# One tile of the cross-attention's probabilities turned by VectorE through DRAM instead of by TensorE

## The chip, the cores and the metric

The kernel runs on one core of one Trainium2 chip. The metric is the device time of one execution in microseconds, here the median of three runs. TensorE is called PE below, VectorE DVE, ScalarE ACT, GpSimd POOL and SyncE SP, as in the rows of the profile.

## The reference

A block of three layers on x of shape (64, 32, 512), with a context of shape (64, 257, 384), everything in float32:

```python
x = x + xattn(layernorm(x), context)   # 16 heads of 64: softmax(q k^T / 8) v, then w_o and a bias
x = x + attn(layernorm(x))             # 16 heads of 32, causal, with a decay by distance
x = x + ffn(layernorm(x))              # 512 -> 2048 -> 512, piecewise-linear GELU, rounded to 2^-8
```

The change lies in the first layer. For each of the 64 batches ("contexts"), 16 heads x 32 queries make 512 rows of scores over 257 keys. The kernel computes scores against the context itself (the key weights are folded into the queries), takes the softmax, and mixes the context rows by the probabilities; the value and output weights come behind that.

## The kernel before, in words

All matmuls are in two float32r pieces, a high and a low part of each operand, and three products (high x high, high x low, low x high). Every engine has a program of its own, written out by hand in order; semaphores join them. No scheduler moves anything.

Cross attention goes by groups of eight contexts (`GB = 8`, eight groups). At a group's boundary the queries are projected and the group before gets its value projection. Within it each context b is one turn of the loop on all five engines. Its 512 score rows are four tiles of 128 (`NT = 4`, 16 heads in fours). In one turn:

- PE: `scores(b, 0)` and `scores(b, 1)`, with `turn_probs(b - 1, 1)` between them, `scores(b, 2)`, `scores(b, 3)`, `mix(b - 1, 0)`, `turn_probs(b, 0)`, `mix(b - 1, 1)`, `mix(b - 1, 2)`. `turn_probs(b, half)` (L911) turns two tiles of probabilities by four 128x128 transposes into a PSUM bank; `mix` (L926) takes the turned probabilities `probt` as one operand. The first, second and last context of a group have a slightly different order.
- DVE: `top` (maximum of a score tile, L1283), `invert` (reciprocal of its sum, L1291), `turn_context` (L1260: 32x32 block transposes of the next context, which lie in `blocks_in`), the low parts of the turned context, of the probabilities (`low_probs`, L1296) and of the mix.
- ACT: the exponentials (`exponent`, L1096) and the high parts (`high_turned`, `high_probs`, `high_mix`, `high_context`).
- POOL: `low_context` (L786), `scale` (L791: multiplies a tile of exponentials by its reciprocal, in place), `shift` (L780), and in five contexts of a group the split of one 128x512 block of the FFN's weights (L797 to L801), which goes through DRAM (`ffn`).
- SP issues every transfer: `load_context` (L613), `load_odd` (L619), the FFN blocks (L639 to L650), and `load_blocks` (L603): four reads that bring the context's 32x32 blocks to where DVE's block transpose makes a full transpose of them. `load_blocks(b + 2)` is issued in turn b and used by DVE's `turn_context(b + 2, 0)` in turn b + 1, right behind `top(b + 1, 0)`.

SP's order in a turn is written in this loop:

```python
if b + 2 < B:
    load_context(b + 2)
for j in ffn_block_of(b + 1) if b % GB == 0 else ffn_block_of(b) if b % GB > 1 else ():
    load_ffn_block(j)
if b + 2 < B:
    if b % GB > 0:
        load_blocks(b + 2)
    load_odd(b + 2)
```

## Time and profile before

| | |
|---|---|
| median of three runs | 1588.15 us (1588.05 to 1588.57) |
| the profiled execution | 1588.07 us |
| its span in the profile | 1586.2 us |
| PE busy | 1570.0 us, 99% |
| DVE, ACT, POOL busy | 1243.0, 1020.1, 816.3 us |
| granted PE clock | full speed over the whole span (2.4 GHz) |

The span is the time from the first to the last instruction; some 2 us of the execution lie around it. A timeline row gives the start in us from the span's start, the duration in us, the engine, the line and the operation; neighbours of one kind are merged (x4) and the idle time before stands in square brackets where there was some. PE's matmuls are pipelined, so durations overlap and the distance between starts is what one takes. Cross attention's groups run from about 110 to 900 us of the span.

### The profile page before, as it was taken

The page shows a single profiled execution, that of the slowest core. Times are in us where ns is not written, and L with a number is a line of the kernel's source. Part 1 is how long each engine was busy: PE and PEld are TensorE (multiplying, and loading weights), DVE is VectorE, ACT ScalarE, POOL GpSimd, SP SyncE. Part 2 cuts the span into 40 slices and gives each one's busy share as a digit, 9 for nine tenths or more (in the row PEclk, how much of TensorE's full clock was granted, in tenths as well). Part 3 has the DMA queues.
Part 4 walks back from the last instruction along what each step waited for, and adds up shares of the span by engine and source line. Part 5 has one row for each costly group of instructions (what it writes and reads, how often), then busy time and mean ns, then how long its engine had stood idle before and what let it go on. Part 6 is the DMA issues. An engine that isn't in the chain of part 4 may idle for free. (4 is left out here: it accounts for less than half of the span.)

```text
span 1586.2 us, 30382 instructions
## 1 busy us (share of the span) xinstructions
PE 1570.0 (99%) x11114; PEld 1376.8 (87%) x11114; DVE 1243.0 (78%) x2411; ACT 1020.1 (64%) x2025; POOL 816.3 (51%) x780
## 2 busy tenths in 40 slices
PE   9999999999999999999999999999999999999998
PEld 7889899898999989999899888988988887888886
DVE  6558878787888878878788685767777889989887
ACT  3457777777777777777787442445446666676765
POOL 3317657376573856747455232334334555555554
PEclk9999999999999999999999999999999999999999
DMA  8984636456364654635443684432436601010010
GB/s 253 273 256 150 179 112 186 128 168 178 116 185 120 179 164 128 184 111 151 140 111 95 188 285 138 133 93 80 137 94 228 238 14 61 20 43 31 14 48 27
DMA packets 203412, 215.60 MB, mean 136 GB/s; under 512 B 83776, under 2 KB 149632, under 8 KB 203264
## 3 DMA queue, kind: packets, MB, share of 16 engines
q1 hardware_dynamic: 203264, 213.66, 44.3%
q8 instruction: 89, 1.46, 0.4%
q14 instruction: 59, 0.48, 0.1%
HBM read 154.88 MB, written 58.72 MB: 135 GB/s over the span
## 5 line engine op out<-in xcount | busy, mean ns | idle before, releaser
L79 PE MATMUL p_bank_score<-p_ctxt,p_qo 128*128 128x256 f32 x2304 | 304.5, 286 | 0.7 <-ACT p_probs L1105 0.3
L79 PEld LDWEIGHTS p_bank_score<-p_ctxt,p_qo 128*128 128x128 f32 x2304 | 288.1, 191 | 5.8 <-issue 2.1
L79 PE MATMUL p_bank_mix<-p_probt,p_ctx 128*128 128x512 f32 x1152 | 292.1, 398 | 0.5
L79 PEld LDWEIGHTS p_bank_mix<-p_probt,p_ctx 128*128 128x128 f32 x1152 | 207.4, 189 | 41.9 <-issue 3.8
L1307 DVE SCALAR_TENSOR_TENSOR p_qo<-p_bank_mix,p_odd,p_qo 128x512 fp32r<-128x512 f32 x192 | 143.8, 749 | 57.7 <-ACT p_qo L1119 50.1
L1119 ACT ACTIVATE p_qo<-p_bank_mix,p_odd 128x512 fp32r<-128x512 f32 x192 | 132.3, 689 | 68.1 <-PE p_bank_mix L79 67.7
L1105 ACT ACTIVATE p_probs<-p_bank_score,p_small 128x257 f32<-128x257 f32 x256 | 121.3, 475 | 59.6 <-DVE p_small L1288 55.6
L794 POOL TENSOR_SCALAR p_probs<-p_probs,p_small 128x256 f32<-128x256 f32 x256 | 121.4, 480 | 71.3 <-DVE p_small L1294 71.2
L788 POOL TENSOR_TENSOR p_ctx<-p_ctx_in,p_ctx 128x768 fp32r<-128x768 f32 x64 | 118.3, 1848 | 68.1 <-ACT p_ctx L1094 67.7
L783 POOL TENSOR_TENSOR p_ctx_in<-p_ctx_in,p_odd_in 128x768 f32<-128x768 f32 x64 | 118.1, 1846 | 40.7 <-DMA p_odd_in<-in_ctx_dram 40.7
L1288 DVE TENSOR_REDUCE p_small<-p_bank_score 128x1 f32<-128x257 f32 x256 | 105.3, 414 | 10.7 <-PE p_bank_score L79 7.9
L79 PE MATMUL p_bank_mm<-p4a_zt,p_wattn 128*128 128x256 f32 x768 | 96.0, 285 | 0.5 <-PEq L1454 0.3
L1278 DVE SCALAR_TENSOR_TENSOR p_ctxt<-p_bank_turn,p_odd_minus,p_ctxt 128x256 fp32r<-128x256 f32 x192 | 87.0, 481 | 12.1 <-ACT p_ctxt L1084 11.7
L79 PEld LDWEIGHTS p_bank_mm<-p4a_zt,p_wattn 128*128 128x128 f32 x768 | 93.0, 191 | 1.8 <-issue 0.5
L1837 POOL TENSOR_TENSOR p_pieces_k<-p_pieces_k 128x512 f32<-128x512 f32 (+1 forms) x33 | 52.5, 1591 | 75.8 <-ACT p_pieces_k L2060 75.8
L1084 ACT ACTIVATE p_ctxt<-p_bank_turn,p_odd_minus 128x256 fp32r<-128x256 f32 x192 | 83.5, 470 | 10.5 <-DVE p_bank_turn L1272 8.3
L771 POOL CAST p_qo<-p_probs 128x512 fp32r<-128x512 f32 x32 | 19.5, 610 | 134.6 <-ACT p_probs L1142 134.6
L1837 POOL TENSOR_TENSOR p_pieces_q<-p_pieces_q 128x512 f32<-128x512 f32 x32 | 52.1, 1629 | 69.4 <-ACT p_pieces_q L2060 69.4
L1272 DVE STREAM_TRANSPOSE p_bank_turn<-p_blocks_in 128x256 f32<-128x256 f32 x192 | 78.6, 440 | 3.2 <-DMA p_blocks_in<-in_ctx_dram 2.9
L1301 DVE TENSOR_TENSOR p_probt<-p_bank_probt,p_probt 128x512 fp32r<-128x512 f32 x112 | 75.6, 675 | 0.2
L79 PE MATMUL p_bank_mm<-p5a_zt,p_wattn 128*128 128x512 f32 x288 | 71.5, 397 | 0.0
L949 PE MATMUL p_bank_score<-p_qo,p_wv 128*64 128x256 f32 x312 | 70.1, 284 | 0.6
(302 smaller groups left out, 3910.7 us busy)
## 6 DMA issues: line engine op xcount, KB each, us to landing
p_blocks_in<-in_ctx_dram SPq DMA_DIRECT2D x256, 96.0 KB, 2.4
p_ctx_in<-in_ctx_dram SPq DMA_DIRECT2D x64, 384.0 KB, 3.2
q<-p_ctx SPq DMA_DIRECT2D x64, 256.0 KB, 3.6
ffn<-p_w_raw SPq DMA_DIRECT2D x64, 256.0 KB, 3.0
p_odd_in<-in_ctx_dram SPq DMA_DIRECT2D x64, 192.0 KB, 3.6
p_x<-in_x_dram SPq DMA_DIRECT2D x32, 256.0 KB, 4.2
p_quad<-q SPq DMA_DIRECT2D x32, 256.0 KB, 3.7
p_probt<-q SPq DMA_DIRECT2D x32, 256.0 KB, 3.9
```

Source lines behind the costliest of these rows:

```text
L79: made = e.matmul(out, lhsT, rhs, start=n == 0, stop=n == last)
L783: e.tensor_tensor(ctx_in[b % 2][:], ctx_in[b % 2][:], odd_in[:, None, :].to_broadcast([P, SP, CC]), ALU.subtract).then_inc(shifted, 1)
L788: e.tensor_tensor(ctx[b % 2][:, LO], ctx_in[b % 2][:], f32(ctx[b % 2][:, HI]), ALU.subtract).then_inc(ctx_lo, 1)
L794: e.tensor_scalar(probs[n % 6][:, 0:KEYS], probs[n % 6][:, 0:KEYS], small[n % 4][:, 2:3], 1.0, ALU.mult, ALU.mult).then_inc(normal, 1)
L1084: e.activation(ctxt[b % 2][:, HI, k, :], b_turn[:, (k % 2) * KEYS:(k % 2 + 1) * KEYS], ACT.Identity, bias=odd_minus[:, k, b:b + 1]).then_i ...
L1105: e.activation(probs[n % 6], b_score[n % NS][:, 0:S], ACT.Exp, bias=small[n % 4][:, 0:1], accum_out=small[n % 4][:, 1:2]).then_inc(exped, 1)
L1119: e.activation(qo[:, HI, m, b % GB, :, :].rearrange("p h t -> p (h t)"), b_mix[m], ACT.Identity, bias=odd[:, m, b:b + 1]).then_inc(out_hi, 1)
L1272: e.transpose(b_turn[:, (k % 2) * KEYS:(k % 2 + 1) * KEYS].rearrange("p (i c) -> p i c", c=QUAD), blocks_in[:, :, k, :]).then_inc(turned, 1)
L1278: e.scalar_tensor_tensor(out=ctxt[b % 2][:, LO, k, :], in0=b_turn[:, (k % 2) * KEYS:(k % 2 + 1) * KEYS], scalar=odd_minus[:, k, b:b + 1], ...
L1288: e.tensor_reduce(small[n % 4][:, 0:1], b_score[n % NS][:, 0:S], AX, ALU.max, negate=True).then_inc(topped, 1)
L1307: e.scalar_tensor_tensor(out=lo, in0=b_mix[m], scalar=odd[:, m, b:b + 1], in1=f32(hi), op0=ALU.add, op1=ALU.subtract).then_inc(out_lo, 1)
L1837: e.tensor_tensor(a[:, at], a[:, at], g0[:, at], ALU.subtract).then_inc(sloped, 1)
```

## The change

In the second to seventh context of each group (`is_moved`, 48 of 64) tile 0 of the probabilities is no longer turned by PE. `scale(b, 0)` writes it, with its columns in another order, to a buffer (`moving`, which lies over the low half of `probt`). SP puts it to DRAM (`put_rows`), waits for that to land, and reads it back in four transfers (`move_blocks`) that bring its 32x32 blocks to where one DVE block transpose (`turn_moved`) makes a full transpose of them, in the next context's turn. ACT takes its high part (`high_moved`) and POOL its low part (`low_moved`). PE's `turn_probs` does only tile 1 in half 0, and `mix` takes its six products in another order, the ones with the low probabilities last, behind a wait of their own. `move_blocks(b)` stands ahead of `load_blocks(b + 2)` in SP's program.

```diff
         def sync(e):
...
+            def put_rows(b):
+                e.wait_ge(normal, b * NT + 1)
+                e.dma_start(p_dram[b % 2], moved_from(b)).then_inc(rows_put, DMA)
+
+            def move_blocks(b):
+                e.wait_ge(rows_put, DMA * moves(b))
+                for q in range(NQD):
+                    e.dma_start(moved_to(b)[q * QUAD:(q + 1) * QUAD, :].rearrange("r (h n) -> r h n", h=HT),
+                                p_dram[b % 2, :, q * SP * QUAD:(q + 1) * SP * QUAD].rearrange(
+                                    "(h r) n -> r h n", r=QUAD)).then_inc(blocks_moved, DMA)
...
                     for j in ffn_block_of(b - 1) if b % GB > 0 else ():
                         store_ffn_block(j)
+                    if is_moved(b):
+                        put_rows(b)
                     if b + 2 < B:
                         load_context(b + 2)
                     for j in ffn_block_of(b + 1) if b % GB == 0 else ffn_block_of(b) if b % GB > 1 else ():
                         load_ffn_block(j)
+                    if is_moved(b):
+                        move_blocks(b)
                     if b + 2 < B:
                         if b % GB > 0:
                             load_blocks(b + 2)
...
         def gpsimd(e):
...
+                to, made = probs[n % 6][:, 0:KEYS], probs[n % 6][:, 0:KEYS]
+                if tile == 0 and is_moved(b):
+                    e.wait_ge(mixed, KC * (b - 1))
+                    to = moved_from(b).rearrange("p (q s k) -> p s q k", s=SP, k=QUAD)
+                    made = made.rearrange("p (s q k) -> p s q k", s=SP, k=QUAD)
+                e.tensor_scalar(to, made, small[n % 4][:, 2:3], 1.0, ALU.mult, ALU.mult).then_inc(normal, 1)
+
+            def low_moved(b):
+                e.wait_ge(moved_hi, moves(b))
+                e.tensor_tensor(probt[b % 2][:, LO, :, 0:P], turned_to(b), f32(probt[b % 2][:, HI, :, 0:P]),
+                                ALU.subtract).then_inc(moved_lo, 1)
...
                 low_context(b)
+                if is_moved(b - 1):
+                    low_moved(b - 1)
...
         def tensor(e):
...
-                for i in range(2):
+                for i in (1,) if half == 0 and is_moved(b) else (0, 1):
...
-                    e.wait_ge(probt_lo, 2 * (b + 1))
+                    e.wait_ge(probt_hi, 2 * (b + 1))
+                    if is_moved(b):
+                        e.wait_ge(moved_hi, moves(b))
...
+                for h in (HI, LO):
+                    for s in range(SP):
+                        e.matmul(b_mix[m], ctx[i][:, h, s, cols], probt[i][:, HI, s, :], start=h == HI and s == 0,
+                                 stop=False)
+                if m == 0:
+                    e.wait_ge(probt_lo, 2 * (b + 1))
+                    if is_moved(b):
+                        e.wait_ge(moved_lo, moves(b))
+                for s in range(SP):
+                    made = e.matmul(b_mix[m], ctx[i][:, HI, s, cols], probt[i][:, LO, s, :], start=False,
+                                    stop=s == SP - 1)
...
         def scalar(e):
...
+            def high_moved(b):
+                e.wait_ge(blocks_turned, moves(b))
+                e.activation(probt[b % 2][:, HI, :, 0:P], turned_to(b), ACT.Copy).then_inc(moved_hi, 1)
...
                     exponent(b, 0)
+                    if is_moved(b - 1):
+                        high_moved(b - 1)
...
         def vector(e):
...
+            def turn_moved(b):
+                e.wait_ge(blocks_moved, DMA * NQD * moves(b))
+                e.transpose(turned_to(b).rearrange("p s (h r) -> p h s r", r=QUAD),
+                            moved_to(b).rearrange("p (h s k) -> p h s k", s=SP, k=QUAD)).then_inc(blocks_turned, 1)
...
                     else:
+                        if is_moved(b - 1):
+                            turn_moved(b - 1)
                         if not first:
                             low_probs(b - 1, 1)
```

How it moves the instructions on SP, in one ordinary context's turn. Before (L648 and L650 store an FFN block, L616 is `load_context`, L644 `load_ffn_block`, L609 `load_blocks`, L622 `load_odd`):

```order
L648 DMA ffn<-p2_w_raw1 128x512
L650 DMA ffn<-p2_w_raw0 128x512
L616 DMA p2_ctx_in1<-in_ctx_768_dram 128x2x384
L644 DMA p2_w_raw0<-in_L0_ffn_w1_dram 128x512
L609 DMA p2_blocks_in<-in_ctx_768_dram 32x8x96 x4
L622 DMA p2_odd_in<-in_ctx_768_dram 128x384
```

And with the change, where the lines are those of the changed kernel (L679 and L681 the stores, L685 `put_rows`, L690 `move_blocks`, L640 `load_blocks`):

```order
L679 DMA ffn<-p2_w_raw1 128x512
L681 DMA ffn<-p2_w_raw0 128x512
L685 DMA p<-p2_moving0 128x256
L647 DMA p2_ctx_in0<-in_ctx_768_dram 128x2x384
L675 DMA p2_w_raw0<-in_L0_ffn_w1_dram 128x512
L690 DMA p2_probs<-p 32x4x64 x4
L640 DMA p2_blocks_in<-in_ctx_768_dram 32x8x96 x4
L653 DMA p2_odd_in<-in_ctx_768_dram 128x384
```

The put stands ahead of the context's load, and the four reads of the moved blocks stand between the FFN block's load and the four block loads of the next context but one.

On DVE, from the first maximum of a turn on, before (L1272 is `turn_context`, L1301 `low_probs`, L1288 `top`, L1294 `invert`):

```order
L1288 TENSOR_REDUCE p2_small0<-p2_bank_score 128x1
L1272 STREAM_TRANSPOSE p2_bank_turn<-p2_blocks_in 128x256 x2
L1301 TENSOR_TENSOR p2_probt1<-p2_bank_probt,p2_probt1 128x2x256
L1288 TENSOR_REDUCE p2_small1<-p2_bank_score 128x1
L1294 RECIPROCAL p2_small0<-p2_small0 128x1
L1278 SCALAR_TENSOR_TENSOR p2_ctxt1<-p2_bank_turn,p2_odd_minus,p2_ctxt1 128x256 x2
L1288 TENSOR_REDUCE p2_small2<-p2_bank_score 128x1
L1294 RECIPROCAL p2_small1<-p2_small1 128x1
```

And with the change (L1348, L1377, L1364 and L1370 are the same four, L1381 is `turn_moved`):

```order
L1364 TENSOR_REDUCE p2_small0<-p2_bank_score 128x1
L1348 STREAM_TRANSPOSE p2_bank_turn<-p2_blocks_in 128x256 x2
L1381 STREAM_TRANSPOSE p2_moving0<-p2_probs 128x4x2x32
L1377 TENSOR_TENSOR p2_probt0<-p2_bank_probt,p2_probt0 128x2x256
L1364 TENSOR_REDUCE p2_small1<-p2_bank_score 128x1
L1370 RECIPROCAL p2_small0<-p2_small0 128x1
L1354 SCALAR_TENSOR_TENSOR p2_ctxt0<-p2_bank_turn,p2_odd_minus,p2_ctxt0 128x256 x2
L1364 TENSOR_REDUCE p2_small2<-p2_bank_score 128x1
L1370 RECIPROCAL p2_small1<-p2_small1 128x1
```

One more block transpose stands between `turn_context` and `low_probs`, and everything behind it comes later by as much.

On POOL, the first instructions of a turn, with the change (L834 is `low_context`, L849 `low_moved`, L845 `scale`, L829 `shift`):

```order
L834 TENSOR_TENSOR p2_ctx0<-p2_ctx_in0,p2_ctx0 128x768
L849 TENSOR_TENSOR p2_probt1<-p2_moving1,p2_probt1 128x2x128
L845 TENSOR_SCALAR p2_moving0<-p2_probs,p2_small0 128x2x4x32
L845 TENSOR_SCALAR p2_probs<-p2_probs,p2_small1 128x256
L829 TENSOR_TENSOR p2_ctx_in1<-p2_ctx_in1,p2_odd_in 128x768
```

The low part of the tile that was moved in the last turn stands between `low_context` and this turn's first `scale`, where nothing stood before.

## Rows read from the trace of the kernel before

**Rows 1.** The page: busy time by engine, and one group of part 5.

```profile
PE 1570.0 (99%) x11114; PEld 1376.8 (87%) x11114; DVE 1243.0 (78%) x2411; ACT 1020.1 (64%) x2025; POOL 816.3 (51%) x780
...
L922 PE MATMUL p_bank_probt<-ident,p_probs 128*128 128x128 f32 x448 | 67.0, 272 | 0.0
```

**Rows 2.** Timeline of PE: start us, us, engine, line, operation, count.

```profile
527.03 1.24 PE L79 MATMUL p_bank_score<-p_ctxt,p_qo 128*128 128x256 f32 x9
528.11 0.60 PE L922 MATMUL p_bank_probt<-ident,p_probs 128*128 128x128 f32 x4
528.47 3.47 PE L79 MATMUL p_bank_score<-p_ctxt,p_qo 128*128 128x256 f32 x27
531.77 1.55 PE L79 MATMUL p_bank_mix<-p_probt,p_ctx 128*128 128x512 f32 x6
533.17 0.60 PE L922 MATMUL p_bank_probt<-ident,p_probs 128*128 128x128 f32 x4
533.52 2.99 PE L79 MATMUL p_bank_mix<-p_probt,p_ctx 128*128 128x512 f32 x12
536.35 1.24 PE L79 MATMUL p_bank_score<-p_ctxt,p_qo 128*128 128x256 f32 x9
```

**Rows 3.** Timeline of DVE in the same context.

```profile
528.96 0.78 DVE L1272 STREAM_TRANSPOSE p_bank_turn<-p_blocks_in 128x256 f32<-128x256 f32 x2
529.64 0.67 DVE L1301 TENSOR_TENSOR p_probt<-p_bank_probt,p_probt 128x512 fp32r<-128x512 f32 x1
530.24 0.42 DVE L1288 TENSOR_REDUCE p_small<-p_bank_score 128x1 f32<-128x257 f32 x1
530.58 0.15 DVE L1294 RECIPROCAL p_small<-p_small 128x1 f32<-128x1 f32 x1
```

**Rows 4.** Timeline of ACT in the same context.

```profile
529.83 0.84 ACT L1084 ACTIVATE p_ctxt<-p_bank_turn,p_odd_minus 128x256 fp32r<-128x256 f32 x2
530.75 0.48 ACT L1105 ACTIVATE p_probs<-p_bank_score,p_small 128x257 f32<-128x257 f32 x1
```

**Rows 5.** Timeline of POOL, from the group's second context on.

```profile
521.27 0.49 POOL L794 TENSOR_SCALAR p_probs<-p_probs,p_small 128x256 f32<-128x256 f32 x1
...
526.38 0.61 POOL L799 CAST p_w_raw<-p_w_raw 128x512 fp32r<-128x512 f32 x1
527.08 1.30 POOL L801 TENSOR_TENSOR p_w_raw<-p_w_raw 128x512 fp32r<-128x512 f32 x1
528.73 1.84 POOL L788 TENSOR_TENSOR p_ctx<-p_ctx_in,p_ctx 128x768 fp32r<-128x768 f32 x1 [0.36 <-ACT p_ctx L1094]
530.83 0.48 POOL L794 TENSOR_SCALAR p_probs<-p_probs,p_small 128x256 f32<-128x256 f32 x1 [0.25 <-DVE p_small L1294]
532.07 0.48 POOL L794 TENSOR_SCALAR p_probs<-p_probs,p_small 128x256 f32<-128x256 f32 x1 [0.77 <-DVE p_small L1294]
```

**Rows 6.** Timeline of SP's DMA issues (merged, x4 is four issues).

```profile
530.61 0.38 SPq L616 DMA_DIRECT2D p_ctx_in<-in_ctx_dram  x1
...
532.86 1.81 SPq L609 DMA_DIRECT2D p_blocks_in<-in_ctx_dram  x4
```

**Rows 7.** DMA landings: block loads over the span, the last in context 3, one w_raw load.

```profile
DMA to landing us min/median/max: 2.0/2.4/6.6
...
DMA to landing us min/median/max: 2.5/2.6/2.6
...
p_w_raw<-in_L_ffn_w_dram SPq DMA_DIRECT2D x1, 256.0 KB, 4.2
```

**Rows 8.** Timeline of SP in stage two: a row tile put and read back.

```profile
1012.21 0.34 SPq L1703 DMA_DIRECT2D z<-p4a_z  x1
1014.26 1.75 SPq L1712 DMA_DIRECT2D p4a_z<-z  x4
1025.09 0.34 SPq L1703 DMA_DIRECT2D z<-p4a_z  x1
...
1027.83 1.75 SPq L1712 DMA_DIRECT2D p4a_z<-z  x4
```

More of the change, by code:

```diff
@@ L243, in __init__, with cross_attention @@
         self.late_in = room.sem_ring("late_in", 3)
-def cross_attention(nc, kept, stack, ident, ident_ready, x_rows, w_q, w_k, w_v, w_o, b_o, ctx_dram, q_dram, o_dram,
+def cross_attention(nc, kept, stack, ident, ident_ready, x_rows, w_q, w_k, w_v, w_o, b_o, ctx_dram, q_dram, p_dram, o_dram,
                     x1_dram, moments, w_attn, w_proj, w_1, w_2, ffn_dram):
@@ L307, in cross_attention @@
             ctxt = [carve(second, f"ctxt{i}", [P, 2, KC, KEYS], F32R) for i in range(2)]
+            with ExitStack() as between:
+                carve(between, "probt0_high", [P, SP, ROW])
+                moving = [carve(between, "moving0", [P, SP, ROW])]
             probt = [carve(second, "probt0", [P, 2, SP, ROW], F32R)]
+            with ExitStack() as between:
+                carve(between, "probt1_high", [P, SP, ROW])
+                moving.append(carve(between, "moving1", [P, SP, ROW]))
             with ExitStack() as boundaries:
@@ L374, in probs_bank, with is_moved, moves, moved_from @@
             return b_probt
+        def is_moved(b):
+            return 0 < b % GB < GB - 1
+        def moves(b):
+            return b // GB * (GB - 2) + b % GB
+        def moved_from(b):
+            return moving[b % 2][:, 0, 2 * P:2 * P + KEYS]
+        def moved_to(b):
+            return probs[b * NT % 6][:, 0:KEYS]
+        def turned_to(b):
+            return moving[b % 2][:, :, 0:P]
         FIRST_TWO = [(b, 1 + 4 * b) for b in range(2)]
+        def probs_rows(b, half, side):
+            first = P if half == 0 and is_moved(b) else 0
+            return (probt[b % 2][:, side, :, half * 2 * P + first:(half + 1) * 2 * P],
+                    probs_bank(b, half).rearrange("p (s r) -> p s r", s=SP)[:, :, first:2 * P])
         def turned_in(b):
@@ L410, in cross_attention @@
             "probs_turned", "probt_hi", "probt_lo", "mixed", "out_hi", "out_lo")
+        rows_put, blocks_moved, blocks_turned, moved_hi, moved_lo = room.sems(
+            "rows_put", "blocks_moved", "blocks_turned", "moved_hi", "moved_lo")
         queried, qo_hi, qo_lo, qo_mid, qo_pool, valued, o_half, o_whole = room.sems(
@@ L793, in scale @@
                 e.wait_ge(inverted, n + 1)
-                e.tensor_scalar(probs[n % 6][:, 0:KEYS], probs[n % 6][:, 0:KEYS], small[n % 4][:, 2:3], 1.0,
-                                ALU.mult, ALU.mult).then_inc(normal, 1)
+                to, made = probs[n % 6][:, 0:KEYS], probs[n % 6][:, 0:KEYS]
[8 more added lines that the diff above has]
+                                ALU.subtract).then_inc(moved_lo, 1)
             def split_ffn_block(j):
@@ L934, in mix @@
                     e.wait_ge(out_lo, KC * (b - 1) + m + 1)
-                accumulate(e, b_mix[m], [x for s in range(SP) for x in three(
-                    lambda h, s=s: ctx[i][:, h, s, cols], lambda h, s=s: probt[i][:, h, s, :])]
-                ).then_inc(mixed, 1)
+                for h in (HI, LO):
[9 more added lines that the diff above has]
+                                    stop=s == SP - 1)
+                made.then_inc(mixed, 1)
             def add_values(g, t, i, side, ks, bank):
@@ L1099, in exponent @@
                     e.wait_ge(probs_turned, (n - 6) // 2 + 1)
+                if n >= 6 and (n - 6) % NT == 0 and is_moved((n - 6) // NT):
+                    e.wait_ge(blocks_turned, moves((n - 6) // NT))
                 if tile == 0 and b > 0 and b % GB == 0:
@@ L1113, in high_probs @@
                 e.wait_ge(probs_turned, 2 * b + half + 1)
-                e.activation(probt[b % 2][:, HI, :, half * 2 * P:(half + 1) * 2 * P],
-                             probs_bank(b, half).rearrange("p (s r) -> p s r", s=SP), ACT.Copy).then_inc(probt_hi, 1)
+                hi, bank = probs_rows(b, half, HI)
+                e.activation(hi, bank, ACT.Copy).then_inc(probt_hi, 1)
+            def high_moved(b):
+                e.wait_ge(blocks_turned, moves(b))
+                e.activation(probt[b % 2][:, HI, :, 0:P], turned_to(b), ACT.Copy).then_inc(moved_hi, 1)
             def high_mix(b, m):
@@ L1299, in low_probs @@
                     e.wait_ge(o_gone[0], DMA * NT // 2 * (b // GB))
-                hi, lo = (probt[b % 2][:, s, :, half * 2 * P:(half + 1) * 2 * P] for s in (HI, LO))
-                e.tensor_tensor(lo, probs_bank(b, half).rearrange("p (s r) -> p s r", s=SP), f32(hi),
-                                ALU.subtract).then_inc(probt_lo, 1)
+                (hi, bank), (lo, _) = (probs_rows(b, half, s) for s in (HI, LO))
+                e.tensor_tensor(lo, bank, f32(hi), ALU.subtract).then_inc(probt_lo, 1)
+            def turn_moved(b):
+                e.wait_ge(blocks_moved, DMA * NQD * moves(b))
+                e.transpose(turned_to(b).rearrange("p s (h r) -> p h s r", r=QUAD),
+                            moved_to(b).rearrange("p (h s k) -> p h s k", s=SP, k=QUAD)).then_inc(blocks_turned, 1)
             def low_mix(b, m):
@@ L2374, in build @@
     q_dram = nc.dram_tensor("q", [2, INNER, ROWS], F32, kind="Internal").ap()
+    p_dram = nc.dram_tensor("p", [2, P, (S - 1) // P * P], F32, kind="Internal").ap()
     o_dram = nc.dram_tensor("o", [INNER, ROWS], F32, kind="Internal").ap()
@@ L2390, in build @@
                 nc, kept, weights, ident, ident_ready, x_rows, L0_xattn_w_q, L0_xattn_w_k, L0_xattn_w_v, L0_xattn_w_o, L0_xattn_b_o,
-                ctx_768, q_dram, o_dram, x1_dram, x1_moments, L0_attn_w_attn, L0_attn_w_proj, L0_ffn_w1, L0_ffn_w2, ffn_dram)
+                ctx_768, q_dram, p_dram, o_dram, x1_dram, x1_moments, L0_attn_w_attn, L0_attn_w_proj, L0_ffn_w1, L0_ffn_w2, ffn_dram)
             after = FirstProducts(nc, kept, ident, ident_ready, x2_moments)
```

## Prediction

> **What bounds the kernel now.** I read the page first. PE is busy 99% of the span, VectorE 78%, ScalarE 64%, GpSimd 51% [rows 1]: the kernel is as long as PE's instruction stream, and a change helps only if it shortens that stream without making PE wait. Then I read the timeline of one ordinary context, the third of a group, engine by engine, because shares say nothing about which wait is near. PE starts its scores at 527.03 and those of the next context at 536.35 [rows 2]: the pitch is **9.32 us** and PE has no hole in it. What matters is how closely the others follow. VectorE turns the next context's blocks at 528.96, runs low_probs at 529.64, the maximum of tile 1 at 530.24 and the reciprocal of tile 0 at 530.58, with no gap [rows 3]. ScalarE's high_turned starts at 529.83 and the exponential of tile 1 at 530.75 [rows 4]. GpSimd scales tile 0 from 530.83 to 531.31 and tile 1 until 532.55 [rows 5]; PE turns tile 1 at 533.17 [rows 2], so that chain has **0.62 us** of slack. SyncE issues the context's block loads at 532.86, four in 1.81 us [rows 6], and the last lands 2.6 us after its issue [rows 7]: 532.86 + 1.36 (three quarters of 1.81) + 2.6 = 536.8. VectorE needs them one pitch after 528.96, at 538.28. This transfer has 1.5 us of slack, and the change moves work in front of it.
>
> **What PE is rid of.** 48 contexts (six in each of eight groups) lose the two PE transposes of tile 0. Four of them take 528.47 - 528.11 = 0.36 us and 533.52 - 533.17 = 0.35 us from first start to next start [rows 2], so one is worth 0.089 us: 96 x 0.089 = **8.5 us** off PE's stream. The group's row offers two larger values: 67.0 us over 448 is 150 ns, and the mean of one is 272 ns [rows 1]; both count overlap with the neighbours, and the start-to-start time is what PE gives back. The mix does the same six matmuls in another order, and its later wait for the low halves can only help: cost nothing, hidden in the same stream.
>
> **What the others get, beside PE's stream.** VectorE: one more 128x256 transpose, 0.34 us to the next start (0.78 for two, so one lasts 0.44) [rows 3]; low_probs of half 0 is halved and comes late in the context, where it delays nobody, so I count nothing back. ScalarE: high_moved, 256 wide, about 0.47 by the 257-wide exponential's 0.48 [rows 4]. GpSimd: low_moved, a two-input operation 256 wide; 768 wide takes 1.84 and 512 wide 1.30 [rows 5], so 0.54 for each 256 elements and 0.76 for the one. Its bounds are 0.48 (the one-input scale of that width) and 0.92 (half of 1.84). Effect within a context, even if every transfer is early: blocks turned 0.68 + third transpose 0.44 + 0.09 to ScalarE (530.66 to 530.75 [rows 3, 4]) + high_moved 0.47, then high_turned 0.84 and a gap of 0.03, puts tile 1's exponential 2.55 us after VectorE's 528.96 instead of 1.79. Those 0.76 us meet the 0.62 us of slack: 0.14 us is left over. Small, but the slack is gone, so any further lateness of VectorE goes straight to PE.
>
> **What SyncE gets: a loop.** In each of the 48 contexts SyncE now waits for tile 0's scale, puts the rows to DRAM, issues the context and FFN loads, waits until the put has *landed*, issues four moved-block reads, and only then the four block loads that VectorE needs early in the next context. There VectorE's work leads to the next scale of tile 0. So each context starts where the last one's block loads landed. Step by step, from the end of scale(b, 0):
> - to the put's issue: 0.04 (ctx_lo at 530.57, SyncE at 530.61 [rows 5, 6]).
> - put's issue to the first read's: in stage two a tile is put and read back in just this form, 1012.21 to 1014.26 = 2.05 us, and 1025.09 to 1027.83 = 2.74 us behind another load [rows 8]. Here the queue is nearly empty ahead of the put: I take 2.05, with 2.74 as the other end. The context and FFN issues, some 0.4 us each [rows 6], fit inside it.
> - four reads issued: 1.75 [rows 8] plus a gap of 0.05: 1.80; bounds 1.4 (four of 0.34 [rows 8]) and 1.86 (as rows 6).
> - the fourth block load starts 1.36 after the first [rows 6] and lands 2.6 after that [rows 7]; bounds 2.0 (the smallest of all) and 4.2 (a load that was queued behind a context load) [rows 7]. Then 0.05 to VectorE.
> That is 0.04 + 2.05 + 1.80 + 1.36 + 2.60 + 0.05 = **7.90 us** from scale to blocks. From there VectorE turns blocks 0.68, moved rows 0.44, 0.09, high_moved 0.47, 0.07, low_moved 0.76, scale 0.48 [rows 3 to 5]: **2.99 us** (the 0.09 is the gap read above; 0.07 and the 0.05s are estimates for gaps of its kind). Low_moved stands ahead of scale in GpSimd's program, so all of it counts; the path through low_probs, maximum and reciprocal (0.68 + 0.34 + 0.60 + 0.34 + 0.15 and 0.1 to GpSimd = 2.2) is shorter than the 2.5 in front of scale. One turn of the loop: 7.90 + 2.99 = **10.89 us** against a pitch of 9.32: 1.57 us too long.
>
> Over a group: the loop starts in the second context, whose scale ends at 521.76 [rows 5]; VectorE wants the blocks at 528.96, 7.20 us later, and gets them after 7.90: 0.70 late. Five more turns (third to seventh context's scale, then the blocks for the eighth's) add 5 x 1.57: 8.55 us. VectorE has no slack left, so PE is late by as much, plus the 0.14 of above: 8.7 us. PE never catches up, since its stream is dense; and the 8.5 us of transposes it no longer does only lengthen its waits. In the last group no blocks are left to load in the seventh context, one turn fewer. Sum: 8 x 8.7 - 1.57 = **68 us**.
>
> The Trainium skill ("DMA: Bandwidth & Descriptors", Anatomy of one DMA) gives a transfer about 2.0 us plus its bytes over 436 GB/s. By it the 128 KB put would take 2.3 us and a 96 KB block load 2.2 us, an estimate by which the turn is 10.74 us and the sum some 61 us. The rows have 2.05 for a put of 256 KB and 2.6 for the loads; the sum above goes by the rows.
>
> The profiled execution took 1588.07 us (span 1586.2), 0.08 below the median of 1588.15; 1588.07 + 68 = **1656**.
>
> **The rivals.**
> 1. *PE stays the bound: faster.* If the turn came out at 9.13 us or less (pitch less 0.18), nothing would wait and PE would keep the 8.5 us: **1580**. The put and the reads would have to be nearly two microseconds quicker than rows 7 and 8 have them. For it: VectorE, ScalarE and GpSimd all have idle time in total. Against it: the smallest value of each row still makes 0.04 + 2.05 + 1.4 + 1.36 + 2.0 + 0.05 + 2.71 = 9.61. Chance 0.08. The Trainium skill ("TensorE: Matmul & The Clock Gate", Part 4: PE-mode transpose) gives a PE transpose about 275 ns in a kernel; if all of that came back this case would be 96 x 0.275 = 26 us and 1562 us, an estimate; rows 2 speak against it.
> 2. *GpSimd's loop decides: slower by less.* The FFN block load now stands behind the put: issued 0.82 after scale (0.04, the put's 0.34 [rows 8], the context load's 0.38 [rows 6], gaps), landed 4.2 later [rows 7], then cast and difference 2.0 (0.70 and 1.30), low_context 1.84, low_moved 0.76, scale 0.48 [rows 5] and 0.05: 10.15 us a turn. It decides where the block loads land in 2.0 and low_moved takes 0.48. Some 26 turns (four per group, 6.4 groups, since 32 blocks go five to a group) x 0.83 = 21 us: **1609**. Chance 0.15.
> 3. *The transfers collide: slower by more.* With the put at 2.74, because the context and FFN loads (640 KB) follow on its heels, the turn is 11.58 and the first lateness 1.39: 8 x (1.39 + 5 x 2.26 + 0.14) - 2.26 = 100 us: **1688**. Block loads behind the moved reads at 4.2 as well would make 13.2 a turn and about 1760. Chance 0.20.
> 4. *No change.* The 8.5 us and a turn of some 9.5 us cancel: **1588**. Chance 0.02. That the edit does not act is excluded by the order of instructions on SyncE and VectorE.
>
> **How the numbers follow.** Forecast 0.55 at 1656; rivals 0.08, 0.15, 0.20 and 0.02. The range leaves out the faster case and the far end of the third: from 1605, just under rival 2, to 1700, just over rival 3 at the put's measured bound. A measurement of this kernel can tell about 0.2%, 3 us. Faster: 0.08; within: 0.02; slower: 0.55 + 0.15 + 0.20 = 0.90.
>
> **What would show it.** PE's idle time, 16 us now (1586.2 less 1570.0 [rows 1]), grows to 80 to 90 us, in front of the transposes of tile 1 (and some in front of the mix). VectorE's transposes of blocks_in wait for a DMA, 45 us or more in total. SyncE waits at the moved reads for the put, about 1 us in each of 48. Within a group, contexts two to seven run at a pitch of 10.9 us, and the first and last keep theirs. Wrong would be: pitch at or under 9.3 (rival 1), GpSimd's cast waiting for w_raw in every turn (rival 2), a put over 2.6 us (rival 3). If VectorE waits for the moved reads instead of the block loads, the loop is another one than I describe.

## The result and the profile after

The changed kernel takes **1655.23 us** (median of four runs, 1654.22 to 1656.01) beside 1588.19 for the kernel before on the same chip: ratio **1.0421, 95% interval [1.0408, 1.0434]**, slower by 67 us. The prediction was 1656, 68 us more. The profiled execution took 1654.82 us, its span is 1653.0.

The page's part 1 of the changed kernel, answering to [rows 1]:

```profile
PE 1576.9 (95%) x11018; PEld 1366.6 (83%) x11018; DVE 1249.2 (76%) x2459; ACT 1016.1 (61%) x2073; POOL 851.4 (52%) x828
```

PE has 96 matmuls fewer and is 76.1 us idle instead of 16.2. It is even 6.9 us *busier*. The last matmul ahead of a stall is shown with its whole tail, 0.15 us or so of which otherwise lies under the next one. PE stalls 73 times in the two rows below, so that is some 11 us (an estimate). Against experiment 2, which runs the same matmuls without these stalls and has PE busy for 1564.2 us, it is 12.7 us more. So 59.9 us more of idle time and 6.9 us more of busy time make the 66.8 us of span. Where it waits, and who makes it wait (view of the waits: engine, line, releaser, us in total, times, longest):

```profile
ACT p_probt L1189 <- DVE p_moving L1381: 84.0, 47, 3.8
DVE p_bank_turn L1348 <- DMA p_blocks_in<-in_ctx_dram: 68.5, 48, 3.4
POOL p_probt L849 <- ACT p_probt L1189: 61.4, 47, 3.5
PE p_bank_probt L979 <- POOL p_probs L845: 37.4, 47, 0.9
PE p_bank_mix L996 <- ACT p_probt L1189: 22.0, 26, 2.4
```

Read it from the bottom: PE waits 37.4 us for the scale of tile 1 ahead of its transposes and 22.0 us for high_moved ahead of the mix. Both stand behind the second row: VectorE's turn of the context waits for the block loads, 48 times, 68.5 us. It never waits for the moved rows: the view has no such row for `turn_moved` (L1381), and in the turn below it starts right behind the turn of the context.

One turn of the loop, first SyncE (start, duration, line):

```profile
576.35 0.32 SPq L685 DMA_DIRECT2D p<-p_moving  x1
576.72 0.43 SPq L647 DMA_DIRECT2D p_ctx_in<-in_ctx_dram  x1
577.20 0.49 SPq L675 DMA_DIRECT2D p_w_raw<-in_L_ffn_w_dram  x1
578.09 1.75 SPq L690 DMA_DIRECT2D p_probs<-p  x4
579.89 2.62 SPq L640 DMA_DIRECT2D p_blocks_in<-in_ctx_dram  x4
```

then VectorE and GpSimd:

```profile
584.60 0.79 DVE L1348 STREAM_TRANSPOSE p_bank_turn<-p_blocks_in 128x256 f32<-128x256 f32 x2 [1.77 <-DMA p_blocks_in<-in_ctx_dram]
585.29 0.40 DVE L1381 STREAM_TRANSPOSE p_moving<-p_probs 128x256 f32<-128x256 f32 x1
```

```profile
575.84 0.48 POOL L845 TENSOR_SCALAR p_moving<-p_probs,p_small 128x256 f32<-128x256 f32 x1
...
586.22 0.73 POOL L849 TENSOR_TENSOR p_probt<-p_moving,p_probt 128x256 fp32r<-128x256 f32 x1 [1.65 <-ACT p_probt L1189]
586.94 0.47 POOL L845 TENSOR_SCALAR p_moving<-p_probs,p_small 128x256 f32<-128x256 f32 x1
```

The scale ends at 576.32, SyncE puts it at 576.35, the blocks are there at 584.60, 8.28 us later; the next scale ends at 587.41, 2.81 us after that. PE waits twice in this turn, 0.67 us for high_moved ahead of the mix and 0.88 us for the scale of tile 1. With the two tails that is 1.85 us, by which the turn (11.09) is longer than PE's stream of 9.24 (experiment 2):

```profile
580.82 1.24 PE L79 MATMUL p_bank_score<-p_ctxt,p_qo 128*128 128x256 f32 x9
...
586.40 1.17 PE L996 MATMUL p_bank_mix<-p_probt,p_ctx 128*128 128x512 f32 x4 [0.67 <-ACT p_probt L1189]
...
588.91 0.41 PE L979 MATMUL p_bank_probt<-ident,p_probs 128*128 128x128 f32 x2 [0.88 <-POOL p_probs L845]
...
591.91 1.24 PE L79 MATMUL p_bank_score<-p_ctxt,p_qo 128*128 128x256 f32 x9
```

PE's scores of this group's contexts start at 559.51, 570.56, 580.82, 591.91, 602.45 and 613.53: pitches of 11.05, 10.26, 11.09, 10.54 and 11.08, mean 10.80, where it was 9.32. The group's second context takes 8.15 us (8.32 before): the block loads are late only from the first put on.

### The profile page after: what moved, and what is told of

The parts are those of the page before. It is cut to its first block and busy times, and to the rows that moved or that the text cites. A ratio compares the mean times of both kernels' runs of the same rounds, so it can differ in the third digit from the quotient of the medians.

```text
span 1653.0 us, 30718 instructions
## 1 busy us (share of the span) xinstructions
PE 1576.9 (95%) x11018; PEld 1366.6 (83%) x11018; DVE 1249.2 (76%) x2459; ACT 1016.1 (61%) x2073; POOL 851.4 (52%) x828
## 5 line engine op out<-in xcount | busy, mean ns | idle before, releaser
L996 PE MATMUL p_bank_mix<-p_probt,p_ctx 128*128 128x512 f32 x768 | 216.6, 404 | 22.1 <-ACT p_probt L1189 22.0
L1387 DVE SCALAR_TENSOR_TENSOR p_qo<-p_bank_mix,p_odd,p_qo 128x512 fp32r<-128x512 f32 x192 | 143.8, 749 | 46.6 <-ACT p_qo L1193 36.7
L829 POOL TENSOR_TENSOR p_ctx_in<-p_ctx_in,p_odd_in 128x768 f32<-128x768 f32 x64 | 118.1, 1846 | 45.1 <-DMA p_odd_in<-in_ctx_dram 45.1
L834 POOL TENSOR_TENSOR p_ctx<-p_ctx_in,p_ctx 128x768 fp32r<-128x768 f32 x64 | 118.3, 1848 | 40.6 <-ACT p_ctx L1162 40.3
L1348 DVE STREAM_TRANSPOSE p_bank_turn<-p_blocks_in 128x256 f32<-128x256 f32 x192 | 79.1, 442 | 68.8 <-DMA p_blocks_in<-in_ctx_dram 68.5
L845 POOL TENSOR_SCALAR p_probs<-p_probs,p_small 128x256 f32<-128x256 f32 x208 | 98.9, 484 | 61.9 <-DVE p_small L1370 61.9
L1003 PE MATMUL p_bank_mix<-p_probt,p_ctx 128*128 128x512 f32 x384 | 118.9, 391 | 0.0
L1364 DVE TENSOR_REDUCE p_small<-p_bank_score 128x1 f32<-128x257 f32 x256 | 104.2, 412 | 7.3 <-PE p_bank_score L79 7.2
L979 PE MATMUL p_bank_probt<-ident,p_probs 128*128 128x128 f32 x352 | 59.5, 277 | 37.4 <-POOL p_probs L845 37.4
L1919 POOL TENSOR_TENSOR p_pieces_k<-p_pieces_k 128x512 f32<-128x512 f32 (+1 forms) x33 | 52.6, 1594 | 75.8 <-ACT p_pieces_k L2142 75.8
L979 PEld LDWEIGHTS p_bank_probt<-ident,p_probs 128*128 128x128 f32 x352 | 39.5, 140 | 58.2 <-issue 51.5
```

What stands on the lines that cost most here:

```text
L829: e.tensor_tensor(ctx_in[b % 2][:], ctx_in[b % 2][:], odd_in[:, None, :].to_broadcast([P, SP, CC]), ALU.subtract).then_inc(shifted, 1)
L834: e.tensor_tensor(ctx[b % 2][:, LO], ctx_in[b % 2][:], f32(ctx[b % 2][:, HI]), ALU.subtract).then_inc(ctx_lo, 1)
L979: made = e.transpose(bank[:, at:at + P], probs[n % 6][:, s * P:(s + 1) * P], ident[:])
L996: e.matmul(b_mix[m], ctx[i][:, h, s, cols], probt[i][:, HI, s, :], start=h == HI and s == 0, stop=False)
L1003: made = e.matmul(b_mix[m], ctx[i][:, HI, s, cols], probt[i][:, LO, s, :], start=False, stop=s == SP - 1)
L1364: e.tensor_reduce(small[n % 4][:, 0:1], b_score[n % NS][:, 0:S], AX, ALU.max, negate=True).then_inc(topped, 1)
```

## Experiments

Ratios are against the kernel before, run on the same chip beside each. "The change" is the changed kernel.

**1. The block loads ahead of the moved reads.** The loop is cut: the block loads no longer stand behind the put's landing.

```diff
+                    if b + 2 < B and b % GB > 0:
+                        load_blocks(b + 2)
                     if is_moved(b):
                         move_blocks(b)
                     if b + 2 < B:
-                        if b % GB > 0:
-                            load_blocks(b + 2)
                         load_odd(b + 2)
```

> SyncE's four block loads stand ahead of the four moved reads; everything else is the change. Theory (a loop from scale over the put, the moved reads and the block loads to the next scale): the blocks are issued 1.5 us after scale, land 5.6 after it, 1.6 before VectorE asks, and the loop over them is gone. The moved reads land about 7.0 after scale, just in time: about 1588 us, 1580 to 1598, the waits of VectorE for blocks_in under 5 us (68.5 in the change). Rival (the added work of VectorE, ScalarE and GpSimd, or the added traffic, makes PE wait): over 1640. Rival (GpSimd's loop over the FFN block's load): about 1600, with GpSimd's cast waiting for w_raw in four contexts of a group.

Measured: 1618.53 us, ratio 1.0191 [1.0177, 1.0205]. Over half of the loss comes back, not all. VectorE still waits for blocks, 22.3 us instead of 68.5, and GpSimd's cast now waits 29.1 us for the FFN block. The block loads are issued 1.45 us after the put (567.42 to 568.87) instead of 3.55 (566.09 to 569.64 in the change), but they land later than the 2.4 us at the median of [rows 7] (landings of the block loads over the span):

```profile
DMA to landing us min/median/max: 2.0/3.5/7.6
```

The put's loop was the larger half. That it was all of it, as I expected, was wrong.

**2. Everything but the transfers.** Put and reads are left out, and turn_moved turns what lies in the buffer.

```diff
-                    if is_moved(b):
-                        put_rows(b)
...
-                    if is_moved(b):
-                        move_blocks(b)
...
-                e.wait_ge(blocks_moved, DMA * NQD * moves(b))
+                e.wait_ge(normal, b * NT + 1)
```

> The put and the moved reads are left out; VectorE turns the tile as it stands (not normalized, not blocked), so the probabilities of tile 0 are not the reference's in 48 contexts. All the work that the change adds to VectorE, ScalarE and GpSimd stays, and SyncE's program is that of before. Theory (the loop through SyncE is the whole loss): PE gets back the 8.5 us, less 0.14 us in a context: 1580 to 1587 us. Rival (added engine work in VectorE's dense stretch): each context loses a microsecond, 1630 or more.

Measured: 1587.08 us, 0.9993 [0.9983, 1.0002]; the pitch in the middle of a group:

```profile
524.26 1.24 PE L79 MATMUL p_bank_score<-p_ctxt,p_qo 128*128 128x256 f32 x9
...
533.50 1.24 PE L79 MATMUL p_bank_score<-p_ctxt,p_qo 128*128 128x256 f32 x9
...
542.73 1.24 PE L79 MATMUL p_bank_score<-p_ctxt,p_qo 128*128 128x256 f32 x9
```

9.24: the 9.32 of before, less 0.18 for two transposes, plus 0.10 for the work that VectorE, ScalarE and GpSimd got (predicted 0.14). So the engines' new work uses up most of the 8.5 us that PE gives back (1.1 us is left, just above the range of 1580 to 1587 that I had named), but it costs nothing against the kernel before. The 67 us come with the transfers and their place in SyncE's program.

**3. The put stays, the reads don't wait for it.** They fetch rows of the context instead, so what is turned is not the probabilities.

```diff
             def move_blocks(b):
-                e.wait_ge(rows_put, DMA * moves(b))
...
-                                p_dram[b % 2, :, q * SP * QUAD:(q + 1) * SP * QUAD].rearrange(
+                                ctx_dram[b, 0:P, q * SP * QUAD:(q + 1) * SP * QUAD].rearrange(
```

> The put goes out as in the change, but the four moved reads fetch rows of the context input instead, so they need not wait for the put's landing (the probabilities of tile 0 are not the reference's in 48 contexts). Theory (the loop is made of SyncE's issues and the last landing; SyncE is busy issuing during most of the put's flight): only 0.42 us in the four contexts with an FFN load and some 0.9 in the other two come back, 8 x 3.5 = 28 us: 1622 to 1636. Rival (the round trip of the put is what costs): 1.75 us a context, 1590 or less.

Measured: 1636.29 us, 1.03 [1.0286, 1.0314]. Without the wait for the landing 19 us come back, the upper edge of my range. In the turn above the context and FFN issues end at 577.69 and the reads start at 578.09, so SyncE waits only 0.4 us for the put. That holds for the 25 turns with an FFN load; in the other 23 fewer issues cover the put, and it waits about 0.95 us. The view of SyncE's own waits in the changed kernel sums it up:

```profile
SPq L690 <- DMA p<-p_moving: 33.1, 47, 2.1
```

So 33 us of waiting are gone and only 19 us of time come back. I haven't shown where the other 14 go. In this run GpSimd's cast waits 21.5 us for the FFN block instead of 12.9. VectorE still waits 50.8 us for the block loads, since the issues alone keep them late.

**4. The mix's new order alone, in the kernel before.**

```diff
-                    e.wait_ge(probt_lo, 2 * (b + 1))
+                    e.wait_ge(probt_hi, 2 * (b + 1))
...
+                for h in (HI, LO):
+                    for s in range(SP):
+                        e.matmul(b_mix[m], ctx[i][:, h, s, cols], probt[i][:, HI, s, :], start=h == HI and s == 0,
+                                 stop=False)
```

> The kernel before with nothing but the mix's new order of products and its later wait for the low halves. Theory (as predicted: it costs nothing): 1588.2 within 1 us. Rival (another order of operands costs PE, 0.07 us a product group as the distance between starts after a wait suggests): 192 x 0.05 = 10 us slower.

Measured: 1587.78 us, 0.9997 [0.9988, 1.0006]. It costs and brings nothing.

**5. SyncE's part alone, in the kernel before.** PE still turns all four tiles; the put of tile 0, the wait for it to land and four reads of a quarter of its columns into a spare tile are added ahead of the block loads. The reads have 1.75 us of issue time, as in the change.

```diff
+                    if is_moved(b):
+                        put_rows(b)
                     if b + 2 < B:
                         load_context(b + 2)
...
+                    if is_moved(b):
+                        move_blocks(b)
```

> The kernel before, PE turning all four tiles, with SyncE's part alone added: the put of tile 0, and four reads of it (a quarter of the columns, into a spare tile that nobody reads) ahead of the block loads. Theory (SyncE's order closes the loop without any of the added engine work): the turn is 7.5 to 8.3 us from scale to blocks plus 2.35 through turn_context, low_probs, maximum, reciprocal and scale, some 10.2 us against 9.32: 1618 to 1640 us. Rival (the loss needs the added work of VectorE, ScalarE and GpSimd): 1588 to 1592.

Measured: 1635.9 us, 1.0304 [1.0289, 1.0319] and VectorE waits 75.8 us for the block loads, 47 times. Five DMA issues and two waits (for the scale and for the put's landing) ahead of the block loads cost 48 us with no added engine work. The block loads themselves are no slower: they land in 2.5 us at the median here and in 2.4 in the changed kernel, where it was 2.4 before. They are issued too late.

**6. Every other context moved** (contexts 1, 3 and 5 of a group, 24 instead of 48).

```diff
         def is_moved(b):
-            return 0 < b % GB < GB - 1
+            return b % GB in (1, 3, 5)
```

> The change with only the second, fourth and sixth context of a group moved (24, not 48), SyncE in the order of the change. Theory (a loop: a late block load makes the next scale, and with it the next put, late): the loop is cut after every turn, VectorE is late by 0.3 to 1.1 us once per moved context and starts anew: 1600 to 1615 us. Rival (each moved context costs the same by itself): half of the 67 us, 1622.

Measured: 1611.01 us, 1.0148 [1.013, 1.0165]: 23 us. Half the contexts cost a third of the loss; the same price for each moved context would be half, 1622 us. I had 1600 to 1615 for a loop that starts anew after each.

**7, 8. What holds the block loads back once the loop is cut?** Both start from experiment 1. First with the put behind the context and FFN loads, then also with the engines' new work moved off the way to tile 1.

```diff
-                    if is_moved(b):
-                        put_rows(b)
                     if b + 2 < B:
                         load_context(b + 2)
                     for j in ffn_block_of(b + 1) if b % GB == 0 else ffn_block_of(b) if b % GB > 1 else ():
                         load_ffn_block(j)
+                    if is_moved(b):
+                        put_rows(b)
```

and in 8, on VectorE (ScalarE and GpSimd alike):

```diff
-                        if is_moved(b - 1):
-                            turn_moved(b - 1)
                         if not first:
                             low_probs(b - 1, 1)
                         top(b, 1)
+                        if is_moved(b - 1):
+                            turn_moved(b - 1)
```

> As e1_blocks_first, and the put stands behind the context load and the FFN block's load instead of ahead of them. Theory (what was left of e1's loss is GpSimd's loop: its cast waited up to 3.5 us for w_raw, which was issued behind the put and landed after 4.0 us and more in a burst of ten transfers): the FFN load goes out 0.8 us earlier, GpSimd's cast waits under 0.3 us, the block loads land in 3.0 or less: 1588 to 1600 us. Rival (the added traffic as such fills the DMA engines): no better than e1, 1612 or more, with the block loads still at 3.5.

> As e5, and the added work stands where each engine has room: turn_moved behind the maximum of tile 1, high_moved behind the exponential of tile 1, low_moved between the scales of tile 0 and tile 1. Theory (the 0.76 us that the added work puts in front of tile 1's exponential uses up the 0.62 us of slack): PE waits for no scale and the pitch is 9.13 where the transfers are in time: 1580 to 1588 us, faster than before. Rival (the transfers bound it): the same as e5.

Measured: 1623.46 us, 1.0231 [1.0205, 1.0256], and 1626.55 us, 1.0237 [1.0221, 1.0253]. Neither is better than experiment 1. The put now lands in 3.1 us (1.7 ahead of the loads), and the load of an FFN block now waits for the stores of the one before to land, with the block loads behind it (waits of SP's queue, first of these two kernels; in the kernel before they are 5.0 us in 7 and in the changed one 0.9 in 2):

```profile
SPq L675 <- DMA ffn<-p_w_raw: 64.0, 25, 3.9
```

So the edit brought another landing wait in front of the block loads, and neither run can tell what held them back in experiment 1. The block loads land in 2.7 us at the median here, not 3.5, and VectorE still waits for them, 21.2 and 29.0 us. That made me suspect SyncE's own time: in the turn of the changed kernel above the issues of the put, the four reads, the four block loads and the FFN, context and odd rows take 6.0 us, with two stores 7.1.

**9, 10. The four reads issued by ScalarE,** in two gaps of its program, and no longer by SyncE; in 10 with the engines' new work placed as in 8.

```diff
                         high_mix(b - 1, 0)
                         high_probs(b, 0)
...
+                    if is_moved(b):
+                        move_blocks(b, 0)
                     if not first:
                         high_mix(b - 1, 1)
+                        if is_moved(b):
+                            move_blocks(b, 1)
                         high_mix(b - 1, 2)
```

> The four reads of the moved rows are issued from ScalarE's program, two behind high_probs(b, 0) and two behind high_mix(b - 1, 1), where ScalarE stood idle for 0.62 and 0.68 us in the kernel before; everything else is the change. SyncE keeps the put alone (0.33 us). Theory (what is left of the loss once the loop is open is SyncE's own issue time, not the traffic): block loads are issued some 0.4 us later than before, inside their 1.5 us of slack, VectorE never waits for them, and 1584 to 1594 us come out, since turn_moved still stands ahead of low_probs. Rival (the traffic itself: more transfers in flight make every landing slower, whoever issues them): block loads land in 3.5 us and more as in the runs with the block loads first, VectorE waits for them 20 us or more, 1610 to 1625.

> The same with turn_moved behind the maximum of tile 1, high_moved behind the exponential of tile 1 and low_moved between the scales of tiles 0 and 1, so that nothing new stands on the way to tile 1's exponential. Theory (SyncE's issue time): the 8.5 us of transposes begin to show, 1579 to 1587 us, PE's pitch 9.15 to 9.25 us. Rival (traffic): as the run without the reordering, 1610 to 1625, and PE waits in front of the mix instead of in front of the transposes.

Measured: 1646.74 us, 1.0368 [1.0352, 1.0383], and 1628.17 us, 1.0248 [1.0234, 1.0262]. My theory falls; both are even above the range that its rival had. SyncE and ScalarE of experiment 10:

```profile
571.46 1.91 SPq L640 DMA_DIRECT2D p_blocks_in<-in_ctx_dram  x4
```

```profile
572.28 0.31 ACTq L1182 DMA_DIRECT2D p_probs<-p  x1
...
572.62 0.46 ACTq L1182 DMA_DIRECT2D p_probs<-p  x1
...
573.60 0.79 ACTq L1182 DMA_DIRECT2D p_probs<-p  x2
```

```profile
577.70 0.79 DVE L1351 STREAM_TRANSPOSE p_bank_turn<-p_blocks_in 128x256 f32<-128x256 f32 x2 [0.94 <-DMA p_blocks_in<-in_ctx_dram]
```

The block loads are issued 1.4 us after the scale's end (570.06), as soon as VectorE has left their buffer, and still VectorE gets them at 577.70, 4.3 us after the last one's issue has ended (573.37). The reads of the other queue went out beside them. Landings by kind in experiment 10, from 300 to 800 us (KB each, median us; before: 2.4, 3.5 and 3.6 for the first three rows shown):

```profile
p_blocks_in<-in_ctx_dram SPq DMA_DIRECT2D x152, 96.0 KB, 3.8
...
p_odd_in<-in_ctx_dram SPq DMA_DIRECT2D x39, 192.0 KB, 4.4
p_w_raw<-in_L_ffn_w_dram SPq DMA_DIRECT2D x22, 256.0 KB, 4.0
...
p_probs<-p ACTq DMA_DIRECT2D x116, 32.0 KB, 3.9
```

Against 9, experiment 10 also shows what the order of the engines is worth when the moved rows come late: in 9 high_moved stands ahead of tile 1's exponential and waits for turn_moved with all of ScalarE behind it (73.9 us in 47, up to 3.0). In 10 that is 3.9 us in 5.

**11, 12. Packets or neighbours?** Both start from experiment 10. In 11 the reads fetch the same bytes in a quarter of the pieces; in 12 the 384 KB of the context load go behind the block loads.

```diff
-                e.dma_start(moved_to(b)[q * QUAD:(q + 1) * QUAD, :].rearrange("r (h n) -> r h n", h=HT),
-                            p_dram[b % 2, :, q * SP * QUAD:(q + 1) * SP * QUAD].rearrange(
-                                "(h r) n -> r h n", r=QUAD)).then_inc(blocks_moved, DMA)
+                e.dma_start(moved_to(b)[q * QUAD:(q + 1) * QUAD, :],
+                            p_dram[b % 2, q * QUAD:(q + 1) * QUAD, :]).then_inc(blocks_moved, DMA)
```

```diff
-                    if b + 2 < B:
-                        load_context(b + 2)
...
                         if b % GB > 0:
                             load_blocks(b + 2)
+                        load_context(b + 2)
                         load_odd(b + 2)
```

> The reordered run with the reads on ScalarE, but each of the four reads fetches 32 whole rows of 1 KB instead of 128 pieces of 256 B (the same bytes; the tile so arrives in another order than the transpose needs, so what is turned is not the probabilities). Theory A (it is the number of small packets: the run before had 576 more per context on top of 1968, and its block loads took 3.8 us where they take 2.4 without them): block loads land in 2.4 to 3.0 us again and 1582 to 1600 us come out. Theory B (it is the bytes in flight, or the instants at which the transfers meet): block loads stay at 3.5 us or more and the time stays within 8 us of 1628.

> The reordered run with the reads on ScalarE, and load_context (384 KB, needed only a turn later) issued behind the four block loads instead of ahead of them. Theory A (packets in flight ahead of and beside the block loads make them land late, 3.8 us instead of 2.4): with a third of what is in flight out of the way the block loads land in 2.5 to 3.2 us, the FFN load in 3.3 or less, and 1585 to 1605 us come out. Theory B (the two queues are served in turns, whatever stands ahead): the block loads still meet the four reads, stay at 3.5 us or more, and 1620 to 1632 us come out.

Measured: 1616.88 us, 1.018 [1.0165, 1.0195], and 1606.14 us, 1.0107 [1.009, 1.0124]. In 11 the block loads still take 3.6 us at the median of the span (3.7 in experiment 10). The 11 us gained lie between its two ranges, so the number of pieces plays a part, though not in these loads' median: PE's wait for high_moved ahead of the mix falls from 36.7 to 26.8 us. In 12 the block loads take 2.7 and VectorE hardly waits for them any more (waits from 110 to 900 us):

```profile
PE p_bank_mix L986 <- ACT p_probt L1187: 19.9, 28, 2.0
DVE p_moving L1383 <- DMA p_probs<-p: 14.2, 16, 2.1
DVE p_bank_turn L1350 <- DMA p_blocks_in<-in_ctx_dram: 2.2, 5, 0.7
POOL p_w_raw L844 <- DMA p_w_raw<-in_L_ffn_w_dram: 2.0, 4, 0.7
```

The context load ahead of them was most of the second limit, 22 of 40 us; the time is 1 us above what theory A of 12 named (1585 to 1605). What is left is PE's wait for high_moved, 19.9 us in 28 turns (first row). One part of it is that VectorE now waits for the moved reads themselves, 14.2 us in 16 turns; they land in 3.3 us at the median. Another shows on ScalarE, in a good turn and the next:

```profile
562.97 0.79 ACTq L1181 DMA_DIRECT2D p_probs<-p  x2
...
572.26 1.74 ACTq L1181 DMA_DIRECT2D p_probs<-p  x2
...
574.05 0.69 ACT L1191 ACTIVATE p_qo<-p_bank_mix,p_odd 128x512 fp32r<-128x512 f32 x1 [1.10 <-PE p_bank_mix L993]
```

The two issues take 1.74 us instead of 0.79, and what ScalarE has to do behind them is late by 0.4 us (the mark names PE; the issues that end at 574.00 are what the row starts behind). PE's pitch is 9.29 in the turn with the short issue (564.15 to 573.44) and 9.67 in the one with the long (to 583.11), and PE waits 0.34 us for high_moved in it.

No version beats the kernel before: 1606.14 is the best that computes everything, and 1587.08 without any transfer is the same as before.

## Why the prediction was right, point by point

- *The loop is the mechanism.* Experiment 5 makes 48 of the 67 us in a kernel that is otherwise the one before; experiment 2 has all the rest of the change and loses nothing; cutting the loop (1) gives 37 us back. The block loads land in 2.4 us at the median before and after, so in the changed kernel it is their issue that is late. PE's two waits, 37.4 and 22.0 us, are all but 0.5 of its 59.9 us more of idle time. Rival 1, PE as the bound, is refuted by the pitch (10.80 for 9.13 or less), and rival 4, no change, by the time.
- *The term of 7.90 us from scale to blocks.* In two neighbouring turns it is 7.45 and 8.28, and over 47 turns 7.43 to 9.94, mean 8.08: about half of them near 7.5, the others over 8. The put's issue to the first read is 1.74 (576.35 to 578.09), not 2.05, since the put of 128 KB lands in 1.7, where the rows I took were of 256 KB. Rival 3's 2.74 came up in one turn of 48 (2.93; another had 2.52), though the context and FFN loads follow on its heels. The four reads' issue to the block loads' is 1.80, as said. The issue of the four block loads is 1.91 in most turns and 2.4 to 3.4 in 13, where I had 1.81 in every turn; in other turns they land later. So the put was 0.3 too long in my sum, and the block loads' issue and landing were up to 1 us and more too short in half of the turns.
- *The term of 2.99 us from blocks to scale.* 2.81 in the turn shown and within 0.02 of it in all: turn_moved and high_moved start 0.44 apart, low_moved takes 0.73, the scale 0.47. So the turn of 10.89 is met as 8.08 + 2.82 = 10.90: the mechanism is the one forecast, but that the sum is met within 0.01 is luck, since its terms are off by 0.2 to 0.4 both ways.
- *Turn and group.* Mean pitch 10.80 for 10.89, in turns that alternate, which I had not foreseen. From the last scores of one group to those of the next: 509.27 to 614.95 in the changed kernel, 105.7 us, and 477.59 to 575.10 before, 97.5. The seven such distances add 7.5 to 10.5 us each, on average 8.7, as predicted.
- *The sum by the Trainium skill's rule* ("DMA: Bandwidth & Descriptors", Anatomy of one DMA: about 2.0 us plus bytes over 436 GB/s), some 61 us. That section fits its figures to transfers that GpSimd issues, which the prediction leaves out; here SyncE issues them. The trace does not agree with it: the put landed in 1.7 us where the rule gives 2.3, and the block loads in 2.0 to 6.7 (median 2.4) where it gives 2.2. The measured 67 us are nearer to the sum by the rows.
- *Costed at nothing.* The mix's order (experiment 4) and, nearly, the engines' work (experiment 2: 0.10 us a context for 0.14).
- *Rival 2, GpSimd's loop,* is not the longer one but shows: the cast waits 12.9 us in 24 turns for its block, and once the put's loop is cut (experiment 1) it waits 29.1 us, longer than VectorE for the block loads (22.3 us). The prediction's condition for this rival was not right: low_moved stands in both loops, so a shorter one shortens GpSimd's as well (9.87 us against 10.01 with its numbers), and the rival would not have decided.
- *PE's waits* were said to come ahead of the transposes of tile 1 (37.4 us) with some ahead of the mix (22.0); idle time 76 us where I said 80 to 90. The 16.2 of before and the 66.8 of span make 83.0, and the 6.9 us by which PE is busier are the difference. SyncE's wait for the put is 0.4 us in the turns with an FFN load and 0.95 in the others, 0.7 on average, where I named 1 us: I had costed the context and FFN issues inside the put's time, but not subtracted them here.

What I had wrong came after: of six experiments on the loss that stays when the loop is cut (1 and 7 to 11), five came out slower than my theory said and the sixth, 11, between its two; 12 came out 1 us above its range. I took the lateness of the block loads for a matter of when SyncE issues them. It is as much one of what is in flight beside them: the same load lands in 2.4, 2.7, 3.5 or 3.7 us (medians over the span of the kernel before and of experiments 12, 1 and 10). It is not the landing alone, though: with 2.7 us in experiments 7 and 8 VectorE still waited for them.

**Open:** why one turn's issue is held back and the next one's isn't. In experiment 12 an issue of SyncE took 1.64 us (571.88 to 573.52) just while the two of ScalarE took 1.74 (572.26 to 574.00), so it can hit both at once. Open is also how far the number of small packets, as against their bytes, makes the landings longer. Experiment 11 moved the time and hardly the block loads. Not tried: a second buffer for the blocks, which would let them be issued earlier, and the context load behind the block loads with all the reads on SyncE.

## What to carry to other kernels

An engine that issues transfers in order is part of every loop whose transfers it issues: a wait for a landing ahead of an urgent load delays that load by what of the round trip the issues between do not cover (here 0.4 to 0.95 us), and the issues ahead of it by their own time (here 1.75 us for four reads). Compare the sum of one turn with the pitch, not with idle shares; here 10.9 against 9.3 us decided it, while no engine but PE was over 78% busy. And a transfer's price is read beside what will be in flight then: moving a non-urgent 384 KB load behind the urgent ones brought 22 us here, more than any other step once the loop was cut.

## What the runs showed of the hardware

- *Single issues are held back.* An issue of a block load takes 0.45 us at the median but up to 1.9 (the changed kernel; min/median/max in ns; in the kernel before the same issue already went up to 1.7). By what isn't shown:

```profile
L640 SPq DMA_DIRECT2D p_blocks_in<-in_ctx_dram x256: 333/451/1901, 65.4 to 922.4; - x128
```

The engine that issues stands still for it; on ScalarE this holds its arithmetic (experiment 12, 1.74 for two issues).
- *A second issuing queue brought nothing here.* With the block loads ahead of the reads and the engines' work as in the change, the time is 1618.53 us with all transfers on SyncE (experiment 1) and 1646.74 with the reads on ScalarE (9). The reads landed in 2.6 and 3.8 us at the median, the block loads in 3.5 and 3.7.
- *A put of 128 KB lands in 1.7 us with a nearly empty queue and in 3.1 behind 640 KB of loads* (experiments 1 and 7).
